# A joined embedding loop with half stacks, and the q and k projection of units 1 to 7 as three F32R products of parts made by GpSimd

## What is computed

```python
out = jnp.where(is_hot[:, None], hot_emb_w[tok2hot[flat]], cold_emb_w[tok2cold[flat]] @ proj_w.T)
h = out.reshape(...)                                      # 2048 x 512
qkv = jnp.einsum('bsd,od->bso', _layernorm(h), w_project) # q, k, v: 16 heads of 32
att = jnp.einsum('bhqd,bhkd->bhqk', q, k) / math.sqrt(32) # causal, softmax
h = h + jnp.einsum('bsd,od->bso', softmax(att) @ v, w_out)
h = h + ffn(_layernorm(h))                                # router, 2 of 16 experts, shared expert
```

## Time and profile before

| | us |
|---|---|
| median of 3 runs | 1027.39 (1026.65 to 1028.84) |
| profiled execution, its own time | 1029.54 |
| its span | 1027.7 |
| PE busy | 939.7 (91%) |
| DVE busy | 665.9 (65%) |
| ACT busy | 601.4 (59%) |
| POOL busy | 313.0 (30%) |
| mean granted clock of TensorE | 0.964 of full speed |

### The profile page before, as it was taken

The page is one execution under the profiler, slowest core; times in us unless marked ns, Lnnn a source line. Parts: engine busy times, 40 slices in busy tenths (PEclk is TensorE's granted clock), DMA queues, the critical chain, the costliest instruction groups (busy, mean ns, idle before and its releaser), DMA issues.

```text
span 1027.7 us, 21178 instructions
## 1 busy us (share of the span) xinstructions
PE 939.7 (91%) x6811; PEld 684.8 (67%) x6811; DVE 665.9 (65%) x1746; ACT 601.4 (59%) x1306; POOL 313.0 (30%) x320
## 2 busy tenths in 40 slices
PE   6677599999999999999998889899989999999992
PEld 5333458678686867768686678777866666666661
DVE  8975356566675756667576857757866666666660
ACT  7212167777777767677777832231146777777770
POOL 2287210110202011020202005633344377246542
PEclk9679889999999999999999999999999999999996
DMA  6132824151343406233345021171449768845553
GB/s 217 37 90 86 195 59 107 33 123 43 83 114 67 99 4 133 63 83 84 71 96 186 23 84 62 62 287 51 166 144 339 202 123 179 269 89 95 94 70 41
DMA packets 44574, 114.39 MB, mean 111 GB/s; under 512 B 9332, under 2 KB 11380, under 8 KB 42162
## 3 DMA queue, kind: packets, MB, share of 16 engines
q1 hardware_dynamic: 32146, 87.14, 29.2%
q0 software_dynamic: 12320, 25.90, 13.7%
HBM read 53.03 MB, written 25.17 MB: 76 GB/s over the span
## 4 chain that ended last, share of the span: by engine, by line
PE 71%; issue 8%; DVE 7%; DMA 5%; POOL 4%; ACT 3%; POOLq 0%; another core or an unknown queue 0%; ACTq 0%; DVEq 0%
PE psum L528 11%; PE psum L1349 10%; PE psum L498 8%; PE psum L541 7%; PE psum L518 7%; PE psum L1424 6%; PE psum L503 6%; PE psum L1289 5%; DMA out<-xnT,slot_out 4%; PE psum L1273 3%; PE psum L1393 2%; PE psum L1371 2%; PE psum L544 2%; DVE oh_lo L1585 1%; ACT probsT L595 1%
## 5 line engine op out<-in xcount | busy, mean ns | idle before, releaser
L652 DVE CUSTOM_DVE_ANT_0 psum<-psum,mask_row 128x128 f32<-128x128 f32 (+7 forms) x256 | 194.3, 763 | 59.4 <-PE psum L518 57.0
L610 ACT ACTIVATE probs<-psum,nmax 128x128 f32<-128x128 f32 (+7 forms) x256 | 190.4, 744 | 48.6 <-DVE nmax L652 42.7
L528 PE MATMUL psum<-ident,probs 128*128 128x128 f32 x1152 | 172.6, 275 | 4.7 <-ACT probsT L595 3.2
L518 PE MATMUL psum<-k_stack,q_stack 128*128 128x512 f32 (+2 forms) x384 | 155.0, 459 | 19.0 <-issue 9.2
L528 PEld LDWEIGHTS psum<-ident,probs 128*128 128x128 f32 x1152 | 136.1, 140 | 37.0 <-issue 19.0
L595 ACT COPY probsT<-psum 128x512 f32<-128x512 f32 (+3 forms) x256 | 129.0, 504 | 38.0 <-PE psum L528 33.4
L498 PE MATMUL psum<-xnT,w_unit 128*128 128x512 f32 x256 | 131.4, 603 | 0.2 <-ACT full L473 0.2
L445 POOL CAST part_hi<-full 128x512 fp32r<-128x512 f32 x32 | 19.6, 612 | 352.2 <-ACT full L473 247.4
L878 POOL DMA_INDIRECT out<-xnT,slot_out x47 | 82.5, 1756 | 110.6 <-DMA out<-xnT,slot_out 75.8
L518 PEld LDWEIGHTS psum<-k_stack,q_stack 128*128 128x128 f32 x384 | 68.5, 201 | 64.1 <-ACT probs L610 40.9
L1424 PE MATMUL psum<-w_dn,gated_T 128*128 x188 | 88.6, 594 | 1.7 <-ACT gated_T L932 1.7
(11 more groups left out here) (242 smaller groups left out, 1849.6 us busy)
## 6 DMA issues: line engine op xcount, KB each, us to landing
w_gu<-in_wgu SPq DMA_DIRECT2D x16, 1024.0 KB, 7.9
q_stack<-part_hi SPq DMA_DIRECT2D x64, 128.0 KB, 2.4
q_stack<-part_lo SPq DMA_DIRECT2D x64, 128.0 KB, 2.4
k_stack<-part_hi SPq DMA_DIRECT2D x64, 128.0 KB, 2.4
k_stack<-part_lo SPq DMA_DIRECT2D x64, 128.0 KB, 2.4
w_dn<-in_wd SPq DMA_DIRECT2D x16, 512.0 KB, 10.0
out<-acc SPq DMA_DIRECT2D x17, 256.0 KB, 3.7
hot_all<-xn SPq DMA_DIRECT2D x4, 1024.0 KB, 7.9
```

What stands on the lines that cost most here:

```text
L518: mm = pe.matmul(dst[:, c0:c1], qs, k_stack[b][:, h, c0:c1], start=True, stop=True)
L528: mm = pe.transpose(bank(4 + m % 2)[:, (j - 4 * k) * P:(j - 4 * k + 1) * P], probs[n % PSLOTS][:, j * P:(j + 1) * P], ident[:, :])
L610: act.activation(probs[n % PSLOTS][:, 0:(i + 1) * P], bank(2 * (n % 2), 2)[:, 0:(i + 1) * P], ACT.Exp, bias=nmax[:, n % 4:n % 4 + 1], scal ...
L652: dve.tensor_tensor_reduce(out=row, in0=row, in1=mask_row[:, (QT - 1 - i) * P:QT * P], scale=1.0, scalar=3.0e38, op0=ALU.add, op1=ALU.min, ...
```

## The change

- **Projection of units 1 to 7.** POOL splits the normalized rows (`x_hi`, `x_lo`, four chunks of 128 x 512 for each half of a sequence) and the q and k weights (`wq_hi`, `wq_lo`, once for two units), and a piece of q or k is three F32R products. The order of fills becomes q, k of the first half, then q, k of the second, then v. Both part buffers are single.
- **Stacks.** They are loaded in halves of 512 columns, 64 DMAs of 64 KB a unit. `q_stack` and the upper half of k (`k_high`) are single, the lower half of k is double. The lower half is loaded after step 15's scores of the unit before, the upper after its last score.
- **Scores.** For n below 16 four single banks serve, and scores are emitted two steps ahead.
- **Embedding loop.** `LAG` is 2; eleven look-ups stay ahead of the loop and five move into its steps 1 to 5; the fills of unit 0 come in steps 7, 8, 9, 11, 12 and 13 and stay fp32; their parts are made by ACT and DVE straight from PSUM; its stacks are loaded in halves between the stores. ACT, DVE and SP wait for all stores of the embedding before attention. The residual loads of the MoE stage share four semaphores.

```diff
-LAG = 4
+LAG = 2
+EARLY_LOOKS = 11
+FIRST_FILL = {7: 0, 8: 1, 9: 4, 11: 2, 12: 3, 13: 5}
...
+        def score_bank(n):
+            return bank(n % 4) if n < NARROW else bank(2 * (n % 2), 2)
...
+        def stack_half(sp, u, side, half):
+            b = u % 2
+            sp.wait_ge(s_lo, HEAD + 4 * u + 2 * half + side + 1)
...
         def att_sp(sp):
+            for u in range(1, 2 * GROUPS):
+                sp.wait_ge(s_S, HEAD + (u - 1) * STEPS + NARROW)
+                for side in range(2):
+                    stack_half(sp, u, side, 0)
+                if u % 2 and u < 2 * GROUPS - 1:
+                    sp.wait_ge(s_fill, HEAD + FILLS * (u + 1))
+                    load_w(sp, u // 2 + 1)
+                sp.wait_ge(s_S, HEAD + u * STEPS)
+                for side in range(2):
+                    stack_half(sp, u, side, 1)
...
+        def split_rows_in(pool, u, half, c):
+            if u == 1 and half == 0:
+                pool.wait_ge(s_xC, NT)
+            else:
+                v, p = (u, 1) if half else (u - 1, 3)
+                if c < KC - 1:
+                    pool.wait_ge(s_xpused, 6 * (u - 1) + 3 * half - 3 + c + 1)
+                else:
+                    pool.wait_ge(s_fill, HEAD + FILLS * v + p + 1)
...
+            pool.tensor_copy(x_hi[:, c, :], src).then_inc(s_xphi, 1)
+            pool.wait_ge(s_xphi, n)
+            pool.tensor_tensor(x_lo[:, c, :], src, x_hi[:, c, :].bitcast(F32), ALU.subtract).then_inc(s_xplo, 1)
...
+                if side == 0:
+                    pe.wait_ge(s_wqlo, 4 * (u // 2) + k + 1)
+                    pe.wait_ge(s_xplo, 8 * (u - 1) + 4 * half + k + 1)
+                for t, (w, x) in enumerate(((wq_hi, x_lo), (wq_hi, x_hi), (wq_lo, x_hi))):
+                    mm = pe.matmul(bank(7), w[:, k, side * P:(side + 1) * P], x[:, k, :],
+                                   start=(k == 0 and t == 0), stop=(k == KC - 1 and t == 2), skip_group_check=True)
...
+                    if n + 2 < NARROW:
+                        scores(u, b, n + 2)
+                    elif NARROW <= n + 1 < STEPS:
                         scores(u, b, n + 1)
```

282 lines of the change are left out of this document (185 added, 97 removed).

## The result

The changed kernel takes 1014.06 us (median of four runs, 1012.0 to 1014.99); the kernel before took 1028.12 beside it (four runs, 1026.65 to 1029.29). The ratio is 0.9865 with a 95% interval of 0.9847 to 0.9883: 1.35% faster, and 11.6 us slower than forecast, just above the top of the range (1014). The profiled execution took 1012.0 with a span of 1010.2, the fastest of the four; the profiled execution of before, 1029.54, was the slowest of its four. So the trace shows 17.5 us of gain (spans of 1027.7 and 1010.2), the medians 14.1.

The account below looks back on a forecast made before the run. PE was taken to bound units 0 to 6, a chain of latencies unit 7. Gains of 6.2 + 18.2 - 1.8 + 2.3 = 24.9 us gave 1004.6 us profiled and a median of 1002.5, range 986 to 1014.

Parts of the forecast that it names:

- the products and scores: Units 0 to 6: F32R products and scores ahead save 2.6 us a unit, 18.2 us in all.
- the step from trace to median: End of the sum: the median was put 2.15 us below the profiled execution, 1004.6 to 1002.5.
- the head: Before attention: first projection piece at 123.9 instead of 130.1, a gain of 6.2 us (bounds 2 and 11).
- rival D: Steps 12 to 15: GpSimd becomes the bound and the kernel is slower, 1046 us at 3.9 a pair; chance 0.06.
- a unit from 13.8 to 11.2 ... that leaves 2.3: Projection products per unit: 16 pieces save 2.6 us, of which 2.3 remain after waits in steps 17 to 20.
- scores two steps ahead: First sixteen steps of units 0 to 6: four score banks save 0.3 us a unit (bounds 0 and some 1.9).
- so PE waits 0.5 to 0.6 us, three times: Weight loads in units 1, 3 and 5: PE waits for GpSimd's split of chunk 0, costing 1.8 us.
- 17.6, a gain of 2.3: Unit 7's first half falls from 19.9 to 17.6 us with scores ahead (gain bounds 0 and 4.4).
- rival B: Half stacks cost 0.63 us each, 2.7 us late in units 1, 3 and 5: 1010.6 us; chance 0.11.
- it ends long before TensorE needs it: Unit 7: output weights are issued some 20 us after its start, GpSimd's splits still end long before PE needs them.
- Rival C: Copies out of the turning banks take the products' gain, only head and unit 7 are left: 1020.5 us; chance 0.07.

Follow-up runs that it names:

- e3: The changed kernel with GpSimd's split of the output weights in unit 7 held until VectorE has made the inverse sums of rows 5 and 6: 1011.55 us.
- e15: e8 with ScalarE spreading the inverse sums of row 2 alone and the v columns loaded behind the late half stacks: 997.16 us.
- e13: The changed kernel with ScalarE instead of VectorE spreading the inverse sums in all rows, the reciprocal staying on VectorE: 1012.55 us.
- e7: The changed kernel with one fp32 product per q and k piece in units 1 to 7, and no row or weight parts made by GpSimd: 1011.01 us.
- e1: The changed kernel with scores of a unit's first 16 steps issued one step ahead again, four banks and half stacks kept: 1012.78 us.
- e5: The changed kernel with the next group's q and k weight columns loaded and split earlier, the v columns by a separate load: 1006.66 us.
- e8: The changed kernel with e3, e5, e6 and unit 7's late k stack issued during unit 6: 1000.14 us.
- e14: e8 with ScalarE's spread of the inverse sums in place of its held split of the output weights: 998.97 us.
- e6: The changed kernel with GpSimd making the first four weight parts in the head's gaps, ahead of the row parts: 1006.78 us.

## Why the prediction was right and wrong

Against the forecast the products and scores fell 3.3 us short, the load edges cost 4.4 more, unit 7 gave 2.3 less, and the step from trace to median cost 4.2; the head gave 1.7 more and the stage behind attention 1.0 that was not forecast. That is the 11.6 us.

**Right: what bounds, and the head.** TensorE bounds units 0 to 6. Scores start at 113.6 (forecast 114.8, though the steps as listed add up to 42.2 us and not 42.4), the first piece at 122.75 (forecast 123.9) behind 6.8 us of waiting for GpSimd's first weight part (forecast some 6), then a slow stretch. From piece to piece the head gave 7.3, within the bounds of 2 to 11. Its rows:

```profile
122.75 1.62 PE psum L607 x3
...
187.55 0.71 PE psum L607 x3
188.59 0.69 PE psum L607 x3
```

These are the chain's triples: 1.62 us at the slow clock and 0.69 to 0.71 later, as read from the routed stage.

**Right: rival D.** GpSimd's row parts stayed 1.90 us apart and never bound a steady unit. But I read the rule of the Trainium skill, "SBUF — State Buffer", "Who interferes with whom", for GpSimd's side alone, and only over VectorE's two-input operations. There was a plain SBUF to SBUF copy on VectorE, and it was the loser: e3 gives 0.71 us in unit 7, e15 0.33 us a unit.

**Wrong: "a unit from 13.8 to 11.2 ... that leaves 2.3".** The size of a piece was right and the sum was not. I discounted the pieces in steps 17 to 20, and of these the two in row 4 paid in full; the loss lay in steps 12 to 18, where 0.7 us was kept by the copy of inverse sums (e15) and by ScalarE at the drain to two banks (e13). Measured against e7: 1.74. The second term, 0.3 for scores two steps ahead, measures 0.44, but e1 shows that the second step has no part in it. With 2.18 instead of 2.6, and a little less where a unit differs, seven units give 14.9 instead of 18.2.

**Wrong: "so PE waits 0.5 to 0.6 us, three times".** The term was -1.8 and is -6.24 (e5: all of it goes). The load landed after 5.2 to 5.6 us and not 4.4 (before, the three took 4.4, 5.2 and 4.4), and 32 half stacks are now queued right behind it on SyncE, which I take for the reason; that makes the wait 1.2 to 1.6. And I did not price what stands behind it: TensorE, waiting, lost its clock at the first edge, here and in every other profile with this wait, for 1.5 us more. The head's paragraph had the same mechanism and its row; the step of carrying it over to a short wait was missing.

**Wrong: unit 7, "17.6, a gain of 2.3".** The first half did shorten, by 0.17, 0.62 and 0.58 in rows 0 to 2. The next two rows gave back 0.63 and 0.71. The first is at least in part the late stack: its 32 issues fill the 21.6 us from 523.7 to 545.3, and unit 7 has no projection work that would bring step 16 later. (Of the 0.63 us e8 returned 0.34; the rest is open.) That is **rival B's price**, 0.63 an issue; I had taken 0.43 because the DMA share seemed to say transfer time. Half the bytes took the same issue time, so it was issue spacing. (The Trainium skill, "SBUF — State Buffer", "Door 1: The DMA port swizzle", would have led me to an estimate of 0.30; the measurement decides.) Its place was wrong in both texts, units 1, 3 and 5: the last late stack of unit 5 landed at 431.78 and was first used at 434.83, in units 1 and 3 there were 2.7 and 1.4 us to spare, so these units hid it. The load waits ahead of them helped: with those gone, TensorE waits for it in unit 3 (0.56 us in e5, 1.40 in e14). The second is GpSimd's split of the output weights. I had written that it ends long before TensorE needs it, true, and never asked beside what it would run: before, it began 7 us into the unit, beside the short rows, and now 21 us into it (551.95), beside the wide ones.

**Wrong: from trace to median.** 2.15 us below the profiled execution, I said, as before. The median after lies 2.06 above its profiled execution. An offset between one execution and the median is chance, not a property of the kernel; it cost 4 of the 11.6 us.

**Rival C**, the product gain eaten by the copies out of the turning banks, at 1020.5 us (its terms give 1020.7), did not come true: 1.74 us a unit stayed. Yet e7 shows that in sum the products brought nothing, by another path: as much was spent in waits for their parts.

## What to carry to other kernels

An operand that another engine must prepare is only as cheap as its latest delivery: count its first use behind every reload and every stage boundary, and ask whether the source buffer is free earlier than the code assumes (e5) and whether the preparing engine had gaps before its other inputs came (e6). Two edits of that kind (6.0 us of load edges, 6.3 us of head) were worth about as much as the change itself. And when an edit moves a side engine's work in time, list what the neighbours do there: a short SBUF to SBUF copy on VectorE, unimportant alone, was lengthened by up to 1.12 us beside GpSimd, and in e3 0.71 us of it was 0.71 us of unit 7.

## What the runs showed of the hardware

- Behind one wait of 1.46 us TensorE's granted clock was 0.55 to 0.60 for 4 us; behind waits of 1.56 and 1.23 us in the same execution it stayed at 1.00. The first place had the slow clock in all eight profiles that have the wait. So a short stall can cost double, and its length alone does not say where.
- A DMA of 32 partitions issued by SyncE takes its queue 0.63 us (5.02 for eight) at 64 KB as at 128 KB.
- VectorE's reciprocal of 128x128 takes 946 ns, of 128x4 173 ns; ScalarE's copy of 128x128 takes 0.29 us and VectorE's 0.23, or up to 1.35 beside GpSimd (e8, unit 4).
